# Dense attention: row and column sums from four float32 strip products instead of six float32r products

## The reference, cut to what matters

```python
h = jnp.maximum(_layernorm(x, axis=-1), 0.0)
Wh = jnp.einsum('bnf,fo->bno', h, W)
a1, a2 = (a[:Fout, 0], a[Fout:, 0])
s1 = Wh @ a1
s2 = Wh @ a2
e = s1[:, :, None] + s2[:, None, :]
e = jnp.where(e >= 0, e, ALPHA * e)
e = jnp.where(adj_matrix[None] == 0, -jnp.inf, e)
attention = jax.nn.softmax(e, axis=-1)
x = x + jnp.einsum('bij,bjo->bio', attention, Wh)
```

## Time and profile before

| what | us |
|---|---|
| median of 3 runs | 2009.61 |
| the three runs | 2008.75, 2009.61, 2011.37 |
| the profiled execution, its own time | 2009.82 |
| its span | 2008.0 |

### The profile page before, as it was taken

The page is one execution under the profiler, slowest core; times in us unless marked ns, Lnnn a source line. Parts: engine busy times, 40 slices in busy tenths (PEclk is TensorE's granted clock), DMA queues, the critical chain, the costliest instruction groups (busy, mean ns, idle before and its releaser), DMA issues. The chain is left out here.

```text
span 2008.0 us, 32449 instructions
## 1 busy us (share of the span) xinstructions
PE 1926.7 (96%) x11950; PEld 1573.4 (78%) x11950; DVE 1256.0 (63%) x2590; ACT 991.6 (49%) x1651; POOL 190.8 (10%) x160
## 2 busy tenths in 40 slices
PE   6999999999999999999999899999999899897998
PEld 6998888888888889888888556758575788686898
DVE  7566665454445545545654677576664688886886
ACT  4554664343333324422323465573736256675996
POOL 1000000000111111011011150000000011100110
PEclk9999999999999999999999899999999999897999
DMA  4201001000100000100101323434332422001232
GB/s 132 74 0 43 0 0 43 0 0 0 42 1 0 0 0 1 33 1 7 78 0 65 134 84 106 150 95 136 124 91 90 127 83 69 13 0 53 85 105 95
DMA packets 82404, 108.39 MB, mean 54 GB/s; under 512 B 7808, under 2 KB 73984, under 8 KB 79488
## 3 DMA queue, kind: packets, MB, share of 16 engines
q1 hardware_dynamic: 82304, 107.04, 16.8%
HBM read 61.79 MB, written 33.55 MB: 47 GB/s over the span
## 5 line engine op out<-in xcount | busy, mean ns | idle before, releaser
L737 ACT ACTIVATE b_gate<-banks,b_bias 128x512 f32<-128x512 f32 (+2 forms) x460 | 295.2, 669 | 368.4 <-PE banks L55 367.5
L53 PE MATMUL banks<-b_xshi,b_whi 128*128 128x512 f32 (+2 forms) x920 | 351.6, 382 | 2.3 <-PEq L308 1.4
L55 PE MATMUL banks<-b_xshi,b_wlo 128*128 128x512 f32 (+2 forms) x920 | 351.3, 382 | 0.0
L54 PE MATMUL banks<-b_xslo,b_whi 128*128 128x512 f32 (+2 forms) x920 | 351.3, 382 | 0.0
L787 DVE CAST b_xshi<-HT 128x512 fp32r<-128x512 f32 (+3 forms) x130 | 57.4, 484 | 273.5 <-PE banks L55 268.1
L53 PEld LDWEIGHTS banks<-b_xshi,b_whi 128*128 128x128 f32 x920 | 172.7, 188 | 35.6 <-issue 3.1
L55 PEld LDWEIGHTS banks<-b_xshi,b_wlo 128*128 128x128 f32 x920 | 172.7, 188 | 32.6
L54 PEld LDWEIGHTS banks<-b_xslo,b_whi 128*128 128x128 f32 x920 | 172.7, 188 | 32.2
L53 PE MATMUL banks<-b_hshi,b_whi 128*128 128x512 f32 (+2 forms) x512 | 194.4, 380 | 0.0
L55 PE MATMUL banks<-b_hshi,b_wlo 128*128 128x512 f32 (+2 forms) x512 | 194.4, 380 | 0.0
L54 PE MATMUL banks<-b_hslo,b_whi 128*128 128x512 f32 (+2 forms) x512 | 194.4, 380 | 0.0
(11 more groups left out here) (333 smaller groups left out, 3954.2 us busy)
## 6 DMA issues: line engine op xcount, KB each, us to landing
a_xt<-in_x SPq DMA_DIRECT2D x16, 512.0 KB, 4.3
h_scratch<-HT SPq DMA_DIRECT2D x4, 2048.0 KB, 7.0
l_x<-in_x SPq DMA_DIRECT2D x16, 512.0 KB, 3.4
l_w<-h_scratch SPq DMA_DIRECT2D x16, 512.0 KB, 5.2
x_scratch<-l_x SPq DMA_DIRECT2D x16, 512.0 KB, 3.3
c_x<-x_scratch SPq DMA_DIRECT2D x32, 256.0 KB, 3.7
c_relu<-c_vals SPq DMA_DIRECT2D x8, 1024.0 KB, 9.2
x_scratch<-c_x SPq DMA_DIRECT2D x32, 256.0 KB, 2.4
```

The lines of the kernel that those rows point to most:

```text
L53: nc.tensor.matmul(out, w_hi, x_hi, start=first, stop=False)
L54: nc.tensor.matmul(out, w_hi, x_lo, start=False, stop=False)
L55: return nc.tensor.matmul(out, w_lo, x_hi, start=False, stop=last)
L737: nc.scalar.activation(gate[s][:, g, 0:plan.n], pG[s][:, g, 0:plan.n], SIG[g], bias=bias[:, plan.p - 1, 2 * g + s:2 * g + s + 1])\
```

## The change

`rank_rows` makes four float32 products instead of six float32r ones. The weights are 32 columns wide, with W @ a1 in column 0 and W @ a2 in column 1. Each product writes a strip of 32 partitions of `pS`: high half of h by chunk 0, high by chunk 1, low by chunk 0, low by chunk 1. None is added to another in PSUM.

The sum over the four is left to the score product, whose factors now have rank eight. `pick` has two columns per partition: `pick_own` is 1 on partitions 0, 32, 64 and 96, and `pick_other` is 1 on 1, 33, 65 and 97. ScalarE makes `own` = `pS` * `pick_own` + `pick_other` as one 128 x 512 instruction. VectorE makes `other` = `pS` * `pick_other` + `pick_own`, also 128 x 512. VectorE does this as the first instruction of its step, and waits for `own_done` first. The four score products are as they were. The wait of `score` is, too.

In `conv_second` GpSimd no longer clears the wide weights, `own` and `other`, and no longer writes the rows of ones. VectorE makes `pick` by two small reductions of the identity in place of the split of the vectors.

```diff
-                for t in (f32(late.wa_hi[:, :, :]), f32(late.wa_lo[:, :, :]), f32(late.mask[:, :, :]), late.own[:, :], late.other[:, :]):
+                for t in (late.wa_cols[:, :, :], f32(late.mask[:, :, :])):
                     nc.gpsimd.memset(t, 0.0).then_inc(sem["cleared"], 1)
-                pool.wait_ge(sem["cleared"], CLEARED - 2)
-                nc.gpsimd.memset(late.own[S2:S2 + 1, :], 1.0).then_inc(sem["cleared"], 1)
-                nc.gpsimd.memset(late.other[S1:S1 + 1, :], 1.0).then_inc(sem["cleared"], 1)
...
-                    link(V.tensor_copy(late.wa_hi[:, :, pair], late.wa[:, :, :]))
-                    V.tensor_tensor(late.wa_lo[:, :, pair], late.wa[:, :, :], f32(late.wa_hi[:, :, pair]), ALU.subtract)
+                    V.tensor_copy(late.wa_cols[:, :, 0:2], late.wa[:, :, :])
+                    for i in range(2):
+                        V.tensor_reduce(late.pick[:, i:i + 1], late.ident[:, i:P:SLOTS], AX.X, ALU.add)
...
-                    for k in range(KD):
-                        last = mm3(nc, flat, wa_hi[:, k, :], wa_lo[:, k, :], hi[:, k, :], lo[:, k, :], k == 0, k == KD - 1)
+                    for i, half in enumerate((hT_hi[b % 2], hT_lo[b % 2])):
+                        for k in range(KD):
+                            strip = slice((KD * i + k) * SLOTS, (KD * i + k + 1) * SLOTS)
+                            last = nc.tensor.matmul(flat[strip, :], wa_cols[:, k, :], f32(half[:, k, :]), start=True, stop=True)
                     last.then_inc(sem["rank_mm"], 1)
...
                     act.wait_ge(sem["rank_mm"], g + 1)
-                    for row, r, copied in ((S1, own, "own_done"), (S2, other, "other_done")):
-                        nc.scalar.activation(r[row:row + 1, :], pS[row:row + 1, :, :].rearrange("p t r -> p (t r)"), ACT.Copy)\
-                            .then_inc(sem[copied], 1)
+                    nc.scalar.activation(own[:, :], pS[:, :, :].rearrange("p t r -> p (t r)"), ACT.Identity, bias=pick_other,
+                                         scale=pick_own).then_inc(sem["own_done"], 1)
...
+                    dve.wait_ge(sem["own_done"], g + 1)
+                    V.tensor_scalar(other[:, :], pS[:, :, :].rearrange("p t r -> p (t r)"), pick_other, pick_own, ALU.mult,
+                                    ALU.add).then_inc(sem["other_done"], 1)
                     if exists(g + 2) and not (isinstance(g, int) and g == 0):
                         add_x(g + 2, b + 2)
```

More of the change, by code:

```diff
@@ L35 @@
 MASK = -2.0 ** 127
-S1, S2 = 0, 32
 def wait(eng, sem, value):
@@ L134, in __init__ @@
         self.w_hi, self.w_lo = sb("l_w_hi", [P, KD, D], F32R), sb("l_w_lo", [P, KD, D], F32R)
-        self.wa_hi, self.wa_lo = sb("l_wa_hi", [P, KD, P], F32R), sb("l_wa_lo", [P, KD, P], F32R)
+        self.wa_cols, self.pick = sb("l_wa_cols", [P, KD, SLOTS]), sb("l_pick", [P, 2])
         self.mask = sb("l_mask", [P, GT, P], F32R)
@@ L2009, in conv_second @@
         _, again, _ = row_buffers(H1)
-        CLEARED = 7
+        CLEARED = 2
         with nc.Block() as block:
@@ L2080, in last_weights @@
                 def last_weights():
-                    pair = slice(S1, 2 * S2, S2)
                     dve.wait_ge(sem["cleared"], CLEARED)
                     dve.wait_ge(sem["folds"], 2)
-                    link(V.tensor_copy(late.wa_hi[:, :, pair], late.wa[:, :, :]))
-                    V.tensor_tensor(late.wa_lo[:, :, pair], late.wa[:, :, :], f32(late.wa_hi[:, :, pair]), ALU.subtract)
+                    V.tensor_copy(late.wa_cols[:, :, 0:2], late.wa[:, :, :])
+                    for i in range(2):
+                        V.tensor_reduce(late.pick[:, i:i + 1], late.ident[:, i:P:SLOTS], AX.X, ALU.add)
                     for h in range(TILE_GRAPHS):
@@ L2192, in dense_attention @@
         sb, ps = allocator(nc, ctx)
-        ident, ident_r, w_hi, w_lo, wa_hi, wa_lo, mask = (late.ident, late.ident_r, late.w_hi, late.w_lo, late.wa_hi, late.wa_lo,
-                                                          late.mask)
+        ident, ident_r, w_hi, w_lo, wa_cols, mask = (late.ident, late.ident_r, late.w_hi, late.w_lo, late.wa_cols, late.mask)
+        pick_own, pick_other = late.pick[:, 0:1], late.pick[:, 1:2]
         g2, be2, own, other = late.cols["g2"], late.cols["be2"], late.own, late.other
@@ L2305, in rank_rows @@
                 def rank_rows(g, b):
-                    hi, lo = hT_hi[b % 2], hT_lo[b % 2]
                     pe.wait_ge(sem["h_lo"], g + 1)
```

## The result

| | median, us | runs |
|---|---|---|
| before | 2011.37 | 2008.75 to 2013.15, 5 runs |
| changed | 2022.21 | 2021.41 to 2026.92, 5 runs |

The ratio is 1.0063, with a 95% interval of 1.0052 to 1.0074. The changed kernel is slower by 0.63%, some 12.7 us, or 12.6 against the median of 2009.61 that the prediction started from. Forecast were 2025.2 us and a range of 2019 to 2028. The profiled execution took 2024.39 us, its span is 2022.6.

A forecast was written before the change was run, and what follows sets the result against it. TensorE was taken to bound the kernel at 9.47 us a step; a ring of waits would then set 10.69. Thirteen steps give 15.9 us, less 0.5 at the start, plus 0.2 at the end: 2025.2 us by the median, range 2019 to 2028.

The forecast's parts named there:

- TensorE's part: Four strip products in place of six in TensorE's step: 1.83 us becomes 1.52 plus 0.1, saving 0.2 us a step.
- Its idle time: TensorE waiting ahead of score and ahead of rows, 1.4 us a step in all.
- The ring: Waits own, other, add_x, measure, scores, exponential to probT, next own, without TensorE: 10.69 us, 1.22 over the old pace.
- the hand-over: Time from ScalarE's own to the start of VectorE's other, taken as 0.04 us.
- The second ring: Loop through TensorE: other, scores, lo_halves, rows, turn_prob, strips, own; 10.29 us, also above the old pace of 9.47.
- The start: Last layer up to own(1), where TensorE sets the end: two shorter score parts gain 0.5 us.
- Everything ahead of 1834 us: The program before that time in the profile was to stay unchanged.
- 1 (TensorE stays the bound): Loop: order does not matter, pace 9.25 us, kernel 3 us faster at 2006.6; chance 0.05.
- 2: TensorE: the four strips run one after another, 2.5 us a step more, 40 us in all, 2050; chance 0.03.
- 3: Loop: TensorE's idling drops its clock to the lower level, up to 117 us more, 2127; chance 0.02.
- 4 (a much shorter ring through overlap): Loop: overlap between neighbours on ScalarE and VectorE leaves only 13 x 0.6 = 8 us, 2017; chance 0.05.

The follow-up runs named there:

- the last experiment: Kernel before (six products, one-row copies) with VectorE's other ahead of own, turn_prob ahead of rows, three project tiles ahead of score: 2009.88 us, 9.46 us a step.
- e7_half_add_out: Changed kernel with VectorE's add_out made for only two of its four tiles: 2025.46 us, pace 10.49 us a step.
- e10_pe_order_alone: Changed kernel with only TensorE's order altered, turn_prob ahead of rows and three project tiles ahead of score: 2026.64 us in one run, 10.49 us a step.
- e2_behind_add_x: Changed kernel with VectorE making other behind add_x, ahead of measure, instead of first in its step: 2012.24 us, 9.80 us a step.
- e1_order_alone: Kernel before with only the one-row copy to other moved to the head of VectorE's step, waiting for own_done: 2022.26 us, 10.31 us a step.
- e3_other_first: Changed kernel with other made as soon as the strips are done and ScalarE's own waiting for other_done: 2007.84 us, 9.47 us a step.

## Why the prediction was right

The mechanism, the side and the range held; the size was 3 us too large. By its steps:

- **TensorE's part** was right: 1.52 us as in the earlier trace rows and 0.1 for the change of width; the last experiment gave 0.21 us a step. Its idle time was sized at 1.4 us a step and the waits seen are 0.97; the pace doesn't hang on it.
- **The ring** had the right members in the right order. Its length was 10.69 worked out and 10.49 measured. Own was 0.76 (0.78 worked out), the hand-over 0.04. Other lasts 0.81, longer than all its rows, but VectorE starts `add_x` 0.73 after other's start, and 0.73 is what 0.68 and the gap of 0.05 made. The prediction got this sum right by luck, from two parts that were both off.
- **The term that was too large** is the copying of spans that held a wait or hid an overlap. From the exponential to own it took 4.46 us out of the earlier trace rows; in the changed kernel it is 1905.82 - 1901.43 = 4.39. In the earlier trace rows own started when TensorE's six products were done, not when ScalarE was free, so 0.07 of it was waiting for TensorE. From `add_x` to the scores it took 3.28 + 0.03; now it is 1900.07 - 1896.84 = 3.23, since VectorE's small instructions overlap when nothing is waited for. The two are 0.15, and with 0.02 for own and 0.01 lost in rounding 0.18 a step, 2.4 us in 13 steps. From own(1) to own(14) a step is 1.03 us longer than before, not 1.22.
- **The second ring** was right in kind: with the first ring opened, own waited for the strips and the pace was 10.25. That this is near the 10.29 of the prediction is in part luck: with measured members the sum is 10.17, and the run had ScalarE's later copy in it.
- **The start** was sized at 0.5 us of gain and measured at 1.8 in the profiled execution, own(1) being 1.8 us nearer to the layer's first `second_norm`. This isn't settled by the profile. Executions with the same order up to there differ by more than a microsecond, with the moment at which the clock rises: in the changed kernel and in e7_half_add_out own(1) is 25.8 and 27.1 us after that instruction. From 1854 to 1856 the granted clock is 0.74 in the one and 0.50 in the other.
- **Everything ahead of 1834 us** was to be unchanged, and was in its work, the preparation apart. But the last layer starts 2.5 us later in the profiled execution of the changed kernel. The clock's share of this is seen in the second layer. The first row is the changed kernel, the second the one before, columns as in the earlier trace rows:

```profile
1377.60:1384.00 6.40, 6.40 (x116) 5.88 (x115) 2.08 (x3) 0.60 (x1) 0.00 (x0) 0.50 0.12 41
```

```profile
1377.80:1384.00 6.20, 6.20 (x184) 5.72 (x185) 3.06 (x5) 1.20 (x2) 0.00 (x0) 1.00 0.27 90
```

At the same place TensorE runs at half its clock in one and at its full clock in the other, in a part of the program that the change doesn't touch: 116 products in 6.4 us against 184 in 6.2. It isn't the change that does it. From 1377.6 to 1384 e10_pe_order_alone has a clock of 0.50 and e7_half_add_out one of 1.00, with the same code up to the last layer. And the first `second_norm` of the last layer starts at 1833.5 us in e2_behind_add_x, with the preparation of the changed kernel, and at 1838.8 in e1_order_alone, with that of before. So the two profiled spans differ by 14.6 us: 2.5 from ahead of the layer, -1.8 at its start, 13.4 from the 13 steps, 0.5 at its end.

Of the rivals, 1 (TensorE stays the bound) fell with the pace of 10.49 and TensorE's idle time. Opening the ring alone, in e3_other_first, gave 9.47 and not its 9.25; that took TensorE's new order too. 2 fell with the strips' row in the timeline, 3 with the full clock in the loop. 4 (a much shorter ring through overlap) had the right direction, but overlap and hidden waits together took less than 0.2 us a step off the ring, not 0.6.

The Trainium skill's price for own, in "ScalarE: Activation LUTs", in the section on what a table load costs, an estimate of 0.80 us, lies 0.04 above the 0.76 measured. For other the rule of "VectorE: DVE Perf Modes", section on why PSUM operands drop a tier, holds: nothing here read PSUM at the rate of SBUF (e1_order_alone's plain copy of 512 elements from PSUM took 0.68, against 0.475).

## What to carry to other kernels

When an instruction moves to another engine and waits there for the engine it came from, everything behind it on its new engine is tied to that engine's queue. Follow the waits until they come back to where they began, and add up the lengths: if that ring is longer than the busiest engine's step, it sets the pace, and busy shares won't show it. Before giving up on such a change, look at the order of the two waits. Here turning them round won back the whole microsecond a step. The saved TensorE time was worth something only when TensorE's own order was changed as well: 9.47 us a step became 9.25.

## What the runs showed of the hardware

- VectorE seems to pay for a column operand, as ScalarE does. Over 512 elements from PSUM, an instruction with immediates took 0.674 us, one with one column 0.746, and other with two columns 0.81, steps of 0.07 and 0.06. The three also differ in their arithmetic, so that it is the columns is argued and not tested. The next instruction, `add_x`, starts 0.73 us after other's start, so the two overlap by 0.08.
- Four float32 strip products of 32 columns, eight entries, cost TensorE 1.27 us between full-width products: 0.99 from their start to the next product (1905.34 - 1904.35), 0.17 more ahead of them (0.53 from `turn_prob` to them against 0.36 in the earlier trace rows) and 0.11 behind. Six full-width float32r products of the same 512 columns cost 1.47. The gain in the loop was 0.21 us.
